# Gated attention of the first layer: head variance as one fp32 block product, inverse root on ScalarE, key weights converted later

## The reference

```python
o = o + jax.nn.sigmoid(aug_w[..., None] * vh)
mu = o.mean(-1, keepdims=True)
var = o.var(-1, keepdims=True)
o = (o - mu) * lax.rsqrt(var + EPS)
out = jax.nn.silu(g) * o @ Wout
```

## Time and profile before

| | |
|---|---|
| median of three runs | 1153.18 us (1152.45 to 1153.95) |
| the profiled execution | 1153.5 us, span 1152.2 us |
| PE busy | 1132.0 us (98%) |
| DVE busy | 749.9 us (65%) |
| ACT busy | 537.7 us (47%) |
| POOL busy | 245.2 us (21%) |
| chain that ended last | PE 84%, DVE 7%, SP's queue 5% |
| granted clock of PE | 0.999 of full |

### The profile page before, as it was taken

How to read it: one execution, slowest core, us unless ns; L and a number is a source line. 1 busy time by engine, 2 the same in 40 slices (tenths; PEclk the granted TensorE clock), 3 DMA queues, 4 the chain that set the end, 5 groups by cost and what they waited for, 6 DMA issues and landing times.

```text
span 1152.2 us, 21738 instructions
## 1 busy us (share of the span) xinstructions
PE 1132.0 (98%) x8721; PEld 846.5 (73%) x8721; DVE 749.9 (65%) x1524; ACT 537.7 (47%) x1037; POOL 245.2 (21%) x308
## 2 busy tenths in 40 slices
PE   7999999999999999999999999999999999999997
PEld 5654488776658777777777777777888778887886
DVE  6457478769894666666566666665797875546632
ACT  4234457653222655656565656565554532223421
POOL 2300013266740342121212122221532100000000
PEclk9999999999999999999999999999999999999999
DMA  9759710110305264444444444445710502224211
GB/s 348 262 216 399 283 67 1 39 45 1 110 19 183 39 139 99 92 93 93 92 93 93 92 92 95 92 102 82 108 23 1 83 6 32 37 38 76 34 37 37
DMA packets 325671, 111.57 MB, mean 97 GB/s; under 512 B 301834, under 2 KB 302908, under 8 KB 321348
## 3 DMA queue, kind: packets, MB, share of 16 engines
q1 hardware_dynamic: 324224, 109.11, 37.6%
q10 hardware_dynamic: 1348, 1.09, 0.4%
HBM read 65.59 MB, written 20.97 MB: 75 GB/s over the span
## 4 chain that ended last, share of the span: by engine, by line
PE 84%; DVE 7%; SPq 5%; DMA 1%; issue 1%; ACT 1%; POOL 0%; DVEq 0%; ACTq 0%
PE bank L303 61%; SPq L1881 4%; PE bank L583 2%; PE bank L601 2%; PE bank L1982 2%; PE bank L1998 2%; PE bank L1173 2%; PE bank L259 2%; PE bank L519 1%; PE bank L1195 1%; DVE W L2121 1%; DVE W L2132 1%; PE bank L1140 1%; SPq L334 1%; PE bank L1137 1%
## 5 line engine op out<-in xcount | busy, mean ns | idle before, releaser
L1919 POOL COPY PT<-W 32x512 f32<-32x512 f32 x120 | 84.6, 705 | 306.8 <-DVE W L2132 242.7
L2121 DVE CUSTOM_DVE_ANT_0 W<-bank,W 128x512 f32<-128x512 f32 x128 | 80.8, 688 | 100.6 <-PE bank L1982 97.7
L2216 ACT ACTIVATE K<-bank,vecT 128x512 f32<-128x512 f32 x64 | 43.8, 690 | 163.7 <-PE bank L303 163.7
L2237 ACT ACTIVATE W<-W,low 128x512 f32<-128x512 f32 x128 | 90.7, 710 | 16.9 <-DVE low L2121 16.9
L303 PE MATMUL bank<-xT,wT 128*128 128x512 f32 x384 | 92.4, 390 | 0.3 <-DVE BT L320 0.3
L303 PE MATMUL bank<-Wkv,Wq 128*128 128x512 f32 x384 | 92.6, 395 | 0.0
L303 PE MATMUL bank<-Wkv,ctxT 128*128 128x512 f32 x384 | 92.1, 395 | 0.0
L303 PE MATMUL bank<-ctxT,Wkv 128*128 128x512 f32 x384 | 90.0, 392 | 0.7 <-DVE ctxT L320 0.7
L303 PE MATMUL bank<-Wq,Wkv 128*128 128x512 f32 x384 | 89.6, 389 | 0.0
L303 PE MATMUL bank<-woT,hR 128*128 128x512 f32 x384 | 87.8, 390 | 0.7 <-DVE W_late L3103 0.5
L303 PEld LDWEIGHTS bank<-Wkv,ctxT 128*128 128x128 f32 x384 | 70.8, 188 | 22.3 <-ACT K L2216 5.7
(11 more groups left out here) (378 smaller groups left out, 2136.0 us busy)
## 6 DMA issues: line engine op xcount, KB each, us to landing
PT<-W SPq DMA_DIRECT2D x360, 64.0 KB, 2.1
W<-ctx_turned SPq DMA_DIRECT2D x16, 1024.0 KB, 5.9
W<-in_ctx_dram SPq DMA_DIRECT2D x8, 1024.0 KB, 10.7
ctx_turned<-ctxT SPq DMA_DIRECT2D x8, 1024.0 KB, 7.9
ctx_turned<-W SPq DMA_DIRECT2D x8, 1024.0 KB, 6.8
XT<-in_ctx_dram SPq DMA_DIRECT2D x4, 1024.0 KB, 12.0
XT<-in_L_ffn_wi_dram SPq DMA_DIRECT2D x64, 64.0 KB, 2.1
raw_own<-in_ctx_dram SPq DMA_DIRECT2D x3, 1024.0 KB, 10.8
```

Source lines behind the costliest of these rows:

```text
L1919: pool.tensor_copy(there, here).then_inc(kept_p.s, 1)
L2121: dve.tensor_tensor_reduce(out=PR[:, j, :], in0=bank[:, 4 + j % 4, :], in1=mask, scale=1.0, scalar=3.0e38, op0=ALU.add, op1=ALU.min, accum ...
L2216: act.activation(K[:, m, :], bank[:, n % 4, :], ACT.Identity, bias=pcol("L1_xattn_bk", m)).then_inc(ring_a.s, 1)
L2237: act.activation(PR[:, j, :], PR[:, j, :], ACT.Exp, bias=low[:, j:j + 1], scale=-1.0, accum_out=total[:, j:j + 1]).then_inc(expd.s, 1)
```

## The change

The variance of a block is one fp32 product of the whole block matrix (32 x 32 blocks of 1/32) with the squares, 128 x 512 into bank 5: each value stands already 32 times, with features on partitions. ACT reads it. For blocks 2 to 7 it takes the inverse root from bank 5 (`Abs_reciprocal_sqrt`, epsilon as bias) into an SBUF tile; for blocks 0 and 1 it copies bank 5 to SBUF and takes the root there later (`early_root_a`), in round two, behind all the sigmoids, which are drawn forward into rounds one and two. DVE's normal product reads that tile in SBUF. The instructions of `variance_v`, `deviation_pool`, `widen_a` and `widen_pe` are gone. DVE makes the normal product of block t - 2 in round t, behind the masks (of block 0 at the end of its round t = 2). PE puts the first chunk of a projection ahead of the mean product in its rounds 3 to 5. ACT rounds the key weights in rounds 3 to 6; DVE makes their low halves in rounds t = 3, 5, 6, 7.

```diff
             def mean_of_pe(g):
                 pe.wait_ge(low_o.s, low_o(g))
                 if g:
-                    pe.wait_ge(var_v.s, var_v(g - 1))
+                    pe.wait_ge(var_a.s, var_a(g - 1))
...
             def variance_pe(g):
                 pe.wait_ge(sqr.s, sqr(g))
-                for t in range(C):
-                    ins = pe.matmul(bank[:, 5, 4 * t:4 * t + 4], sq_at(g)[:, t * P:(t + 1) * P], block[:, 0:P:GDV], start=True, stop=True)
-                ins.then_inc(var_pe.s, 1)
+                pe.matmul(bank[:, 5, :], block[:], sq_at(g), start=True, stop=True).then_inc(var_pe.s, 1)
...
             def turn_blocks_pe(g):
                 pe.wait_ge(scaled.s, scaled(g))
-                if g + 2 < G:
-                    pe.wait_ge(ynm.s, ynm(g + 2))
...
# PE's loop
-                    if t == 3:
-                        pe.wait_ge(sg_v.s, sg_v(1))
-                        widen_pe(0)
                     if 1 <= t <= G:
                         attend_pe(t - 1)
-                    if 4 <= t < G + 3:
-                        widen_pe(t - 3)
...
+                    if t == 3:
+                        pe.wait_ge(sg_v.s, sg_v(2))
+                    if 3 <= t < 6:
+                        project_pe(t - 3, range(1))
                     if 1 <= t < 6:
                         mean_of_pe(t - 1)
...
                     if 3 <= t:
-                        project_pe(t - 3)
+                        project_pe(t - 3, range(1, C) if t < 6 else range(C))
...
             def normal_v(g):
-                dve.wait_ge(wide_pe.s, wide_pe(g))
+                if g < 2:
+                    dve.wait_ge(root_a.s, root_a(g))
+                else:
+                    dve.wait_ge(var_a.s, var_a(g))
                 dve.wait_ge(gated.s, gated(g))
-                dve.tensor_tensor(y[:, g % 3, :], y[:, g % 3, :], bank[:, 6, :], ALU.mult).then_inc(ynm.s, 1)
+                dve.tensor_tensor(y[:, g % 3, :], y[:, g % 3, :], root_at(g), ALU.mult).then_inc(ynm.s, 1)
...
# DVE's loop
-                    if 3 <= t:
-                        normal_v(t - 3)
                     for r in range(4):
                         masked_v(t, r)
+                    if 3 <= t:
+                        normal_v(t - 2)
...
                     if t == 2:
                         dve.wait_ge(proj.s, proj(GATE + 7))
-                        key_weights_v(0)
                     if t < 3:
                         gate_last_v(5 + t)
-                    if t in (3, 6, 7):
-                        key_weights_v({3: 1, 6: 2, 7: 3}[t])
-                    if 1 <= t:
-                        variance_v(t - 1)
+                    if t == 2:
+                        normal_v(0)
+                    if t in (3, 5, 6, 7):
+                        key_weights_v({3: 0, 5: 1, 6: 2, 7: 3}[t])
...
                 low_of_v(7)
-                normal_v(5)
+                normal_v(6)
                 quantise_v(4)
-                variance_v(7)
                 for g in (5, 6, 7):
                     add_v(g)
-                    if g < 7:
-                        normal_v(g + 1)
+                    if g == 5:
+                        normal_v(7)
...
+            def variance_a(g):
+                act.wait_ge(var_pe.s, var_pe(g))
+                if g < 2:
+                    act.copy(root_at(g), bank[:, 5, :]).then_inc(var_a.s, 1)
+                else:
+                    act.wait_ge(ynm.s, ynm(g - 1))
+                    act.activation(root_at(g), bank[:, 5, :], ACT.Abs_reciprocal_sqrt, bias=eps[:]).then_inc(var_a.s, 1)
+
+            def early_root_a(g):
+                act.wait_ge(var_a.s, var_a(g))
+                act.activation(root_at(g), root_at(g), ACT.Abs_reciprocal_sqrt, bias=eps[:]).then_inc(root_a.s, 1)
...
# ACT's loop
                     if t <= G:
                         attended_a(t - 1)
-                    if t + 1 < G:
-                        sigmoid_a(t + 1)
-                    if 2 <= t < G + 2:
-                        widen_a(t - 2)
+                    if t == 1:
+                        sigmoid_a(2)
+                    elif t == 2:
+                        sigmoid_a(6)
+                        sigmoid_a(7)
                     if t <= G:
                         square_a(t - 1)
                     if t <= 2:
                         gate_out_a(5 + t)
+                    if t == 1:
+                        for g in (3, 4, 5):
+                            sigmoid_a(g)
+                    elif t == 2:
+                        early_root_a(0)
                     if t >= 5:
                         blocks_a(t - 5)
-                    if t <= C:
-                        key_weights_a(t - 1)
+                    if 3 <= t <= 6:
+                        key_weights_a(t - 3)
+                    if t <= G:
+                        variance_a(t - 1)
+                    if t == 2:
+                        early_root_a(1)
```

More of the change, by code:

```diff
@@ L946, in l0_gated_attention @@
             w = sb(ph, "w2", [P, G, GH])
-            var = sb(ph, "var", [P, 2, GH])
-            half = sb(ph, "mhalf", [P, GH])
+            eps = sb(ph, "eps", [P, 1])
             def xb(h, c, lo, n):
@@ L988, in l0_gated_attention @@
             sq_at = lambda g: W[:, 0, 3, :] if g < 2 else sq[:]
-            wide_at = lambda g: y[:, 2, :] if g < 1 else wide[:]
+            root_at = lambda g: y[:, 2, :] if g < 1 else wide[:]
             by_group = lambda ap: ap.rearrange("f (c g r) -> f (c g) r", c=2, g=G)
@@ L1013, in l0_gated_attention @@
             var_pe = signal("b_var_pe")
[L1014 to L1017, removed]
+            var_a = signal("b_var_a")
+            root_a = signal("b_root_a")
             gated = signal("b_gated")
@@ L1039, in gpsimd @@
                     row_stats_pool(1, g)
-                p(pool.memset(half[:], -0.5))
+                p(pool.memset(eps[:], EPS))
                 p(pool.memset(augw[:], 0.0))
@@ L1073, in gpsimd @@
                         scale_pool(t - 4)
-                    deviation_pool(t - 1)
                     if t == G:
@@ L1099, in gated_pool @@
                                    ALU.mult).then_inc(gated.s, 1)
-            def deviation_pool(g):
-                pool.wait_ge(var_v.s, var_v(g))
-                pool.tensor_tensor(var[:, g % 2, :], var[:, g % 2, :], half[:], ALU.pow).then_inc(rst.s, 1)
             def scale_pool(g):
@@ L1153, in variance_pe, with project_pe @@
                 pe.wait_ge(sqr.s, sqr(g))
-                for t in range(C):
-                    ins = pe.matmul(bank[:, 5, 4 * t:4 * t + 4], sq_at(g)[:, t * P:(t + 1) * P], block[:, 0:P:GDV], start=True, stop=True)
-                ins.then_inc(var_pe.s, 1)
[L1158 to L1174, removed]
+                pe.matmul(bank[:, 5, :], block[:], sq_at(g), start=True, stop=True).then_inc(var_pe.s, 1)
+            def project_pe(g, chunks=range(C)):
+                if 0 in chunks:
+                    pe.wait_ge(ynm.s, ynm(g))
+                    if g:
+                        pe.wait_ge(xsum.s, summed(2, g - 3) if g in (3, 4) else summed(1, g - 1))
+                for c in chunks:
+                    ins = pe.matmul(bank[:, 7, :], y[:, g % 3, c * P:(c + 1) * P], slot(7)[:, c, :], start=(c == 0),
+                                    stop=(c == C - 1), skip_group_check=True)
+                if C - 1 in chunks:
+                    ins.then_inc(proj.s, 1)
             def turn_blocks_pe(g):
                 pe.wait_ge(scaled.s, scaled(g))
-                if g + 2 < G:
-                    pe.wait_ge(ynm.s, ynm(g + 2))
                 if g:
@@ L1346, in tensor @@
                         turn_blocks_pe(t - 5)
-                    if t == 3:
-                        pe.wait_ge(sg_v.s, sg_v(2))
                     if 3 <= t:
-                        project_pe(t - 3)
+                        project_pe(t - 3, range(1, C) if t < 6 else range(C))
                     if 1 <= t <= G:
```

## The result

Before: 1153.35 us median (1152.32 to 1154.87, 22 runs). After: 1154.98 us (1153.18 to 1156.64, 22 runs). The ratio is 1.0014, with a 95% interval of 1.0008 to 1.0020: 0.9 to 2.3 us slower. Forecast were 1152.4 us and a range up to 1154.8. The profiled execution took 1156.3 us, its span is 1155.1 (before: 1153.5 and 1152.2).

What follows compares the result with a forecast made beforehand. PE and DVE were taken as near-equal bounds of the joined loop: no gain by round eight, then 0.15 + 0.65 = 0.8 us behind it, 1153.5 to 1152.7, less 0.3 for the median: 1152.4 us. Range 1149.5 to 1154.8.

Steps and rivals of the forecast that it cites:

- Nothing later in the kernel is changed; it starts as much earlier or later as this chain does: Behind the last normalise at 349.58: everything only shifts with the chain of waits, no term of its own.
- Round three: Joined loop: mean at 253.9, table load 1.28 us, one projection chunk already done; ends 0.7 us earlier than before.
- Round four: Joined loop: DVE 0.9 us late, PE waits 0.4; PE 1.2 us ahead at round six's start, 275.2 for 276.42.
- the collision: Round four: POOL's gate falls onto DVE's normal product, adding 0.8 us; bounds for the product 0.60 and 1.5.
- Rounds five and six: Joined loop: key weights one on DVE behind quantising, 2.06 us; PE's lead goes, round six ends 0.3 us later.
- Rounds seven and eight: Joined loop: last low half about 0.9 us later, PE waits 0.3, missing widening pays 0.45; gain 0.0.
- Behind the loop: After the joined loop: statistics 0.15 us earlier, normalise 0.54 instead of 1.17 gives 0.65; sum 0.8 us.
- A: Joined loop: PE stays the bound; time 1149.4 to 1150.4 us; chance 0.27.
- B: Rounds five to seven: DVE's lateness grows, 1 to 2.5 us over before, 1154.2 to 1155.7; chance 0.12.
- C: Square not in the root's table, so ACT loads tables twice every round, 14 times 1.28 us; 1153 to 1154.5; chance 0.05.

Runs made afterwards that it cites:

- edges of before: Changed kernel with 84 tiny transposes (168 PE instructions) ahead of PE's first work: 1152.73 us, ratio 0.9995 to the kernel before.
- the last experiments: Changed kernel, 84 tiny transposes in front, normal product ahead of masks, key weights one in round three, `normal_v(7)` later: 0.26% faster than the kernel before.
- run 13: Not a follow-up kernel: one of the fourth part's 16 PE runs of 128 short matmuls on `PT`, counted from nought; 1.77 us from first to last start unpaused.
- N = 69: Changed kernel with 69 tiny transposes (138 PE instructions) in front: 1153.90 us, ratio 1.0010 to the kernel before.

## Why the prediction was wrong, step by step

- **"Nothing later in the kernel is changed; it starts as much earlier or later as this chain does": the step that failed.** The code later in the kernel is the same, but not its place in the blocks of 256. Removing 169 PE instructions moved the edges: 2.3 us more of pauses in the profiled pair and 1.0 us of landing, of which 2.27 in all reach the end of the part. The forecast had put this term at nothing, with no other ground than that the lines stay the same. The profile of before had the sign of it (69 packets on an instruction queue, a run with 1.06 us behind "issue"), and I read neither.
- **Round three**: root at 251.09, 1.30 us after the one load of 1.28. The Trainium skill's drain on top of it ("ScalarE: Activation LUTs", "What ACT_TABLE_LOAD costs"), which would have made the next activation start 2.66 us after the load's start, is not in this trace either. Mean at 254.29 for a forecast 253.9, and round four starts 0.46 us earlier than before, for 0.7: low by some tenths.
- **Round four**: the collision came as put, 1.47 us for 0.6 beside POOL's gate (263.86, 1.28 us). Round six starts at 275.48 for a forecast 275.2.
- **Rounds five and six**: the pair of low halves 2.14, PE's linear product at 279.86 for a forecast 279.5, the linear add at 284.38 for 284.2. The experiments confirm it from the other side: with that pair moved to round three, 2.4 us come free.
- **Rounds seven and eight, "gain 0.0"**: relative to the first attended block, round seven starts 0.63 us later than before and round eight 0.65; forecast was 0.3 for the first and nothing for the end. This is the term off inside the loop: PE waits 0.77 and 0.35 us for linear adds, and block seven's root is done 0.5 us later than I had it (normal seven 313.81 for 313.3).
- **Behind the loop**: the normalise at 0.54 for 1.17 came exactly, and the longer wait for POOL ahead of the second one as well (1.07 us for 0.59). Sum of the stretch: 0.28 for 0.8, and the missing half is the 0.5 just named.
- **With the edges of before** the changed kernel took 0.8 us less than the kernel before by the medians (by the ratio's interval, from 1.6 less to 0.5 more), where 0.8 was forecast. That the two figures are equal is luck: the stretch gained 0.28.
- **Rivals.** A did not happen; it needed the relief of DVE that the last experiments gave. B names the right time, 1154.2 to 1155.7, for the wrong reason: DVE's last low half is at 305.90, 0.4 later than before (305.48), and the stretch is shorter, not longer. C is false: one table load.
- **A slip that moves nothing**: the text on the earlier trace rows speaks of the last four rounds of the loop, and the rows show two, six and seven.

## What to carry to other kernels

A change that removes or adds instructions on PE shifts all that follows against its code blocks; where later stages have runs of very short matmuls, compare these stages too, and before you credit a few tenths of a per cent to an edit, pad the old kernel to the same position (here such a comparison was good to about 1 us). When a near-equal second engine stands behind the bound, look for the one round in which work was put on it (here a pair of low halves, 2.1 us) before counting on the work taken off the first.

## What the runs showed of the hardware

- PE waits for code. A code packet is 16384 bytes, one per 256 instructions. In runs that pass 256 PE instructions in 1.77 us an edge late in the run (212 to 253) cost 0.5 to 1.9 us in 37 of 39 cases, an edge at 196 or earlier nothing.
- Behind that stands a time and not a place: PE went on 1.2 us or more after the end of its code packet, at each of 955 edges. How long a pause is follows when the packet comes, which is why it varies at one place from one execution to the next (0.51 and 1.26 us in run 13 of the changed kernel). It also fits two gaps outside the runs, 0.68 us (N = 69) and 0.37 us (before), at edges just behind a run: PE went on 1.4 and 1.2 us after the packet. What the 1.2 us are, and what sets the start of a packet, is open; nothing was run on it.
- A code packet took 0.9 to 2.0 us. Each time one ran amid the small moves of `PT` (0.9 to 1.6 us, 5 profiles), the two or three moves under way took 2.6 to 3.3 us for 2.1, and DVE's wait was 0.7 to 1.2 us longer; in the 9 profiles without it the wait was 1.25 to 1.27. That the packet delays them is inferred from this coincidence.
- DVE's normal product, with both inputs in SBUF, took 1.01 to 1.47 us where it met POOL's gate, and 0.68 without it. Four low halves took 2.48 us in round three, and two of them 2.14 behind the quantising, where POOL scales: their price is where they stand.
- PE's first products run at half pace at first: transposes at 11.3 us took 1.91 us for x8 in the kernel before, and the same at 14.9 us took 1.04. Work in front does not settle when the pace doubles: with the same 84 transposes ahead the x8 took from 1.10 to 1.91 us, and with none at all 1.04 in one profile. The joined loop starts at 233.7 to 236.3 us from one execution to another, so no gain is claimed from it.
